# Graph layer kernel: tile 5 transposed by DMA, two adjacency chunks loaded as halves between transposes, h of tiles 6 and 7 a step earlier

## The reference, cut to what matters

```python
# x: 2048 x 512, adj: 2048 x 2048 (sparse, diagonal filled), weight: 512 x 512
h = maximum(layernorm(x), 0)
h_q = round(minimum(h / a, 1) * 15)                    # 4 bit activations
w_q = round(abs(clip(w_norm / wa, -1, 1)) * 7) * sign  # w_norm: weight, centred and scaled
support = relu(h_q @ w_q * scales)
s_q = round(minimum(support / a2, 1) * 15)
x = x + (adj @ s_q) * scales
h = maximum(layernorm(x), 0)
# attention over listed pairs, masked by an aggregator that is the identity
# for adj without ones: its softmax picks the row itself
x = x + h
```

## Time and profile before

| | |
|---|---|
| median of 3 runs | 151.84 us (151.78 to 152.19) |
| the profiled execution | 152.06 us, span 150.2 us |
| PE busy | 135.2 us, 90% of the span |
| DVE / ACT / POOL busy | 107.8 / 103.4 / 35.1 us |
| the chain that ended last | PE 74%, DVE 7%, issue 6%, DMA 2% |

### The profile page before, as it was taken

The page is one execution under the profiler, slowest core; times in us unless marked ns, Lnnn a source line. Parts: engine busy times, 40 slices in busy tenths (PEclk is TensorE's granted clock), DMA queues, the critical chain, the costliest instruction groups (busy, mean ns, idle before and its releaser), DMA issues.

```text
span 150.2 us, 2087 instructions
## 1 busy us (share of the span) xinstructions
PE 135.2 (90%) x672; PEld 85.5 (57%) x676; DVE 107.8 (72%) x223; ACT 103.4 (69%) x153; POOL 35.1 (23%) x72
## 2 busy tenths in 40 slices
PE   0397999799999999999999999999999999999920
PEld 0393545355555555757484757565666657579920
DVE  0889978699865569996863686686968797765450
ACT  3688785678686779506955999999999779411000
POOL 2565412243040000025100201101010652611010
PEclk9999999999999999999999999999999999999996
DMA  5999999531571780250189899999011021011102
GB/s 150 354 395 419 404 398 392 81 70 37 155 231 39 214 380 0 35 249 0 13 286 412 238 393 373 367 357 343 30 60 70 0 74 70 0 70 70 70 9 72
DMA packets 12925, 27.70 MB, mean 184 GB/s; under 512 B 6128, under 2 KB 6384, under 8 KB 10864
## 3 DMA queue, kind: packets, MB, share of 16 engines
q1 hardware_dynamic: 12624, 27.14, 51.7%
q10 hardware_dynamic: 288, 0.39, 0.8%
HBM read 22.03 MB, written 4.19 MB: 175 GB/s over the span
## 4 chain that ended last, share of the span: by engine, by line
PE 74%; DVE 7%; issue 6%; DMA 2%; ACT 1%; POOL 1%; POOLq 0%; DVEq 0%; ACTq 0%
PE acc L1078 27%; PE acc L1074 25%; PE acc L1040 8%; PE acc L1058 7%; PE acc L1053 6%; DVE st L787 2%; DMA h_iT<-h_i 2%; ACT z_sup L453 1%; DVE h_qT L827 1%; ACT h_i L445 1%; DVE ring L861 1%; POOL rs L582 1%; DVE x_sb L983 1%; DVE mv L792 0%; DVE sup L832 0%
## 5 line engine op out<-in xcount | busy, mean ns | idle before, releaser
L1078 PE MATMUL acc<-sup,lo 128*128 128x512 f32 (+1 forms) x208 | 48.3, 384 | 0.0
L1074 PE MATMUL acc<-sup_h,hi 128*128 128x512 f16 (+1 forms) x208 | 43.7, 363 | 0.0
L1078 PEld LDWEIGHTS acc<-sup,lo 128*128 128x128 f32 x208 | 37.0, 188 | 7.9
L567 POOL TENSOR_SCALAR nm<-mv 128x1 f32<-128x1 f32 (+2 forms) x19 | 13.2, 692 | 96.1 <-DVE ve L797 78.0
L426 ACT ACTIVATE junk<-raw,below 128x2048 uint8<-128x2048 f32 x16 | 31.8, 1988 | 0.0
L1074 PEld LDWEIGHTS acc<-sup_h,hi 128*128 128x128 f16 x208 | 19.4, 98 | 21.4 <-issue 2.9
L843 DVE TENSOR_TENSOR lo<-raw,hi 128x2048 fp32r<-128x2048 f32 x11 | 25.2, 2288 | 7.5 <-ACT hi L418 7.5
L460 ACT ACTIVATE ring<-x_sb,nm 128x512 f32<-128x512 f32 x15 | 10.4, 715 | 20.4 <-POOL nm L567 17.2
L1058 PE MATMUL acc<-sup,lo 128*128 128x512 f32 x64 | 21.7, 450 | 0.0
L418 ACT ACTIVATE hi<-raw 128x2048 f16<-128x2048 f32 x11 | 20.9, 1896 | 0.0
L787 DVE BATCH_NORM_STATS2 st<-x_sb 128x6 f32<-128x512 f32 x29 | 19.4, 688 | 0.4
(11 more groups left out here) (77 smaller groups left out, 82.3 us busy)
## 6 DMA issues: line engine op xcount, KB each, us to landing
raw<-adj_t SPq DMA_DIRECT2D x16, 1024.0 KB, 5.8
out<-ring SPq DMA_DIRECT2D x15, 256.0 KB, 4.7
x_sb<-x SPq DMA_DIRECT2D x3, 1024.0 KB, 13.9
w_sb<-weight SPq DMA_DIRECT2D x4, 258.0 KB, 4.0
x_sb<-x SPq DMA_DIRECT2D x1, 512.0 KB, 5.6
x_sb<-x ACTq DMA_DIRECT2D x1, 256.0 KB, 3.6
x_sb<-x SPq DMA_DIRECT2D x1, 256.0 KB, 4.7
h_iT<-h_i SPq DMA_TRANSPOSE x10, 2.5
```

What stands on the lines that cost most here:

```text
L567: nc.gpsimd.tensor_scalar(nm[:, a:a + m], mv[:, a:a + m, 0], -1.0, None, ALU.mult).then_inc(nm_ready, 1)
L1074: nc.tensor.matmul(bank[:, cols], part(hi, k % PARTS, j), sup_h[:, j, cols], start=(j == 0), stop=False)
L1078: ins = nc.tensor.matmul(bank[:, cols], part(lo, k % PARTS, j), sup[:, j, cols], start=False, stop=(j == T - 1))
```

## The change

It has four parts. (1) TURN = 5: tile 5 is transposed by DMA too, and the loop of transposes on SP starts at tile 5. (2) Chunk 2 of adj, x of tiles 12 to 15 and chunk 3 are no longer issued ahead of all transposes. Chunks 2 and 3 are loaded as halves of 512 KB, with a semaphore for the first half; they go behind the transposes of tiles 5, 6, 8 and 10, and the last quarter of x goes behind that of tile 7. (3) AHEAD = 6: h of tiles 6 and 7 is made one step earlier on ACT, and on DVE the statistics of tile 6 move ahead of quantise_sup(2), and `normalise(6)` ahead of lo_of_piece(4). (4) For the last tile EPS is added to the statistics of the first half, so that POOL takes the root straight from `mv` and the variance instruction goes; and the two final stores change engines: ACT stores the first half, SP the second.

```diff
@@ -48,12 +48,13 @@
     HEADS = 8
     DK = D // HEADS
     EARLY = 2
-    TURN = 6
-    AHEAD = 8
+    TURN = 5
+    AHEAD = 6
     SLOTS = 4
 
     WARM_SUMS, WARM_FIRST, WARM_T = 16, 4, (18, 0)
     RAW = 7
+    HALVED = (2, 3)
     PARTS = 3
     RING = 4
 
@@ -157,6 +158,7 @@
         x_in = [sem(f"x_in{n}") for n in range(len(x_loads))]
         w_in = [sem(f"w_in{k}") for k in range(KD)]
         adj_in = [sem(f"adj_in{b}") for b in range(RAW)]
+        adj_half = [sem(f"adj_half{b}") for b in range(RAW)]
         const_ready = sem("const_ready")
         half_ready = sem("half_ready")
         ident_zero = sem("ident_zero")
@@ -178,6 +180,7 @@
         x_var = sem("x_var")
         var_ready = sem("var_ready")
         nm_ready = sem("nm_ready")
+        last_var = sem("last_var")
         r_ready = sem("r_ready")
         relu_ready = sem("relu_ready")
         nb_ready = sem("nb_ready")
@@ -327,13 +330,19 @@
                     sp.wait_ge(screened, k - RAW + 1)
                 sp.dma_start(raw[:, k % RAW, :], adj_t[k]).then_inc(adj_in[k % RAW], 16)
 
+            def load_half(k, first):
+
+
+                cols = slice(0, CHUNK // 2) if first else slice(CHUNK // 2, CHUNK)
+                sp.dma_start(raw[:, k % RAW, cols], adj_t[k][:, cols]).then_inc(adj_half[k % RAW] if first else adj_in[k % RAW], 16)
+
             def store(t):
 
                 if t < T - 1:
                     sp.wait_ge(out_ready, t + 1)
                 else:
-                    sp.wait_ge(last_out_ready, 1)
-                cols = slice(0, D) if t < T - 1 else halves[0]
+                    sp.wait_ge(last_out_ready, 2)
+                cols = slice(0, D) if t < T - 1 else halves[1]
                 sp.dma_start(out[t * P:(t + 1) * P, cols], ring[:, t % RING, cols]).then_inc(out_stored[t % RING], 16)
 
             for k in range(KD):
@@ -344,15 +353,18 @@
             load_x(3)
             load_adj(1)
             load_x(4)
-            load_adj(2)
-            load_x(5)
-            load_adj(3)
             for j in range(TURN, T):
                 wait_h(sp, j)
                 if j >= TURN + 2:
 
                     wait_hT(sp, j - 2)
                 sp.dma_start_transpose(h_iT[:, j % 2, :, :], h_i[:, j % SLOTS, :]).then_inc(h_turned[j % 2], 16)
+                if j in (5, 6):
+                    load_half(2, j == 5)
+                if j == 7:
+                    load_x(5)
+                if j in (8, 10):
+                    load_half(3, j == 8)
                 if j == 11:
 
                     load_adj(GT)
@@ -405,8 +417,13 @@
             def split_piece(p):
                 k, q = p // 4, p % 4
                 if q == 0:
-                    act.wait_ge(adj_in[k % RAW], 16 * (k // RAW + 1))
+                    if k in HALVED:
+                        act.wait_ge(adj_half[k % RAW], 16)
+                    else:
+                        act.wait_ge(adj_in[k % RAW], 16 * (k // RAW + 1))
                     wait_part_free(act, k)
+                if q == 2 and k in HALVED:
+                    act.wait_ge(adj_in[k % RAW], 16)
                 cols = slice(q * PIECE, (q + 1) * PIECE)
                 nc.scalar.activation(hi[:, k % PARTS, cols], raw[:, k % RAW, cols], ACT.Copy,
                                      accum_out=low[:, p:p + 1]).then_inc(hi_piece, 1)
@@ -524,8 +541,8 @@
                     screen_ones(seen)
                     seen += 1
             assert seen == T
-            act.wait_ge(last_out_ready, 2)
-            act.dma_start(out[(T - 1) * P:, halves[1]], ring[:, (T - 1) % RING, halves[1]]).then_inc(out_stored[(T - 1) % RING], 16)
+            act.wait_ge(last_out_ready, 1)
+            act.dma_start(out[(T - 1) * P:, halves[0]], ring[:, (T - 1) % RING, halves[0]]).then_inc(out_stored[(T - 1) % RING], 16)
             with general(act):
                 one_ahead(act, (g_qk_ready, 1))
                 act.wait_ge(first_stored, 1)
@@ -630,8 +647,9 @@
                 n = FIRST + 1 + s - GT
                 centre(n, *second_ln[s - GT])
                 inverse_root(*second_ln[s - GT])
-            pool.wait_ge(var_ready, FIRST + len(second_ln) - EARLY)
-            inverse_root(T - 1, 1)
+
+            pool.wait_ge(last_var, 1)
+            nc.gpsimd.tensor_tensor(rs[:, T - 1:T], mv[:, T - 1, 1:2], minus_half[:, 0:1], ALU.pow).then_inc(r_ready, 1)
             with general(pool):
                 pool.wait_ge(first_stored, 1)
                 pool.wait_ge(g_var, 1)
@@ -922,20 +940,21 @@
             bound_hT(2)
             bound_hT(3)
             lo_of_piece(2)
+            stats(6)
             quantise_sup(2)
 
-            stats(6)
             normalise(5, stats(7))
             bound_hT(4)
             quantise_sup(3)
             lo_of_piece(3)
             wait_x(8)
             stats(8)
+            last = stats(9)
             bound_hT(5)
             quantise_sup(4)
+            normalise(6, last)
             lo_of_piece(4)
-            normalise(6, stats(9))
             bound_hT(6)
             quantise_sup(5)
             lo_of_piece(5)
@@ -985,15 +1004,20 @@
                     if s == T:
                         dve.wait_ge(x1_ready, a + n + 1)
                         ins = nc.vector.bn_stats(st[:, a + n, :], x_sb[:, t, cols])
+                        if n == 0:
+
+                            dve.wait_ge(dve_chain, step(ins))
+                            ins = nc.vector.tensor_scalar(st[:, a, 2:3], st[:, a, 2:3], float(D) * EPS, None, ALU.add)
+                            step(ins)
                 if s < T:
                     for t in range(a, a + m):
                         dve.wait_ge(x1_ready, t + 1)
                         ins = stats(t)
-                    after = mean_var(step(ins), a, m)
+                    variance(mean_var(step(ins), a, m), a, m)
                 else:
                     dve.wait_ge(dve_chain, step(ins))
-                    after = step(nc.vector.bn_aggr(mv[:, a, :], st[:, a:a + 2, :].rearrange("p h s -> p (h s)")))
-                variance(after, a, m)
+                    nc.vector.bn_aggr(mv[:, a, :], st[:, a:a + 2, :].rearrange("p h s -> p (h s)")).then_inc(last_var, 1)
+                    dve.wait_ge(last_var, 1)
                 if s == T:
                     last_result(a)
                     break
```

## The result

The kernel became slower: 154.31 us (153.86 to 155.17, 4 runs) against 152.01 us (151.78 to 152.33, 4 runs) for the kernel before, a ratio of 1.014 with a 95% interval of 1.011 to 1.017. Forecast were 150.7 us and a range of 149.9 to 152.0. The profiled execution took 154.66 us with a span of 152.9.

A forecast was written before the change was run, and what follows sets the result against it. PE's matmuls were taken to bound the kernel, with gains possible only before PE's steady pace and in the tail. First stage 0.76, root 0.18 and stores 0.2 sum to 1.14 us off 151.84: 150.7 us, range 149.9 to 152.0.

The forecast's parts named there:

- ACT's wait for nb: ACT ahead of h(6): a 1.3 us wait delays piece 4 and z_sup(4), hidden by 0.3 us before PE needs sup_h(4).
- PE's own path to support(6): First stage: PE is free at 28.08 after lo of tile 4 and starts support(6) at about 28.1, 1.1 us ahead.
- tile 5's transpose: First stage: by DMA it lands in 2.5 us, at 24.4, hidden with 0.3 us to spare; support(5) starts 0.56 us ahead.
- Support(4): First stage: with tile 6's statistics moved into DVE's idle time, support(4) starts at 22.35, not 22.89, 0.54 us won.
- Rival (c): Tile 5's DMA transpose takes 4.4 us, support(5) starts 1.1 us behind its old time, kernel 152.5 us; chance 0.04.
- the half load: First half of chunk 2, ahead of tile 6's transpose: lands 3.9 us after issue, at 27.05, the transpose at 27.6.
- the load of x and tile 8: x of tiles 12 to 15 ahead of tile 8's transpose: transpose lands at 33.35, leaving 0.76 us of first-stage gain.
- rival (b): Loads stream at lone pace, 3.6 us a megabyte; tile 8's transpose lands at 34.8, kernel 152.1 to 152.6 us; chance 0.08.
- (a): Rival: x's load takes up to 1 us longer, eating the first stage's gain; kernel 151.2 to 151.7 us; chance 0.22.
- tile 12: First stage after tile 8: only half loads between transposes; landings forecast for tiles 9 to 11, none for tile 12.
- the stores: Tail: exchanging the queues of the two final stores wins 0.2 us, bounds 0 and 0.5.
- the root: Tail: POOL's root, starting straight from the aggregation, begins at about 144.98, 0.18 us won.

## Why the prediction was wrong

**Right.** That the ends lie in the first stage's pace and the tail; that ACT's wait for nb would cost nothing (1.41 us, forecast 1.3, and free); PE's own path to support(6), which I had at 10.0 us behind support(2) and which took 10.02 with chunk 2 in front, where the transposes came in time; tile 5's transpose (2.9, 2.7 and 2.5 us forecast; support(5) won 0.36 us on its start, with 0.56 forecast). Support(4) won 0.31 us and not 0.54, measured from support(2). Rival (c) did not come in after, where no load is ahead of tile 5's transpose, and came to pass when the loads were put back in front: 5.3 us, PE waiting 2.5. The rule of the Trainium skill ("VectorE: DVE Perf Modes", "Rules for kernel authors"), TensorE where a PSUM destination will do, agrees with these runs. Tile 5's 2.9 us by DMA were hidden, but they bought nothing: support(6) came 10.02 us behind support(2) with tile 5 by DMA (chunk 2 in front), and 10.03 with it on PE (loads as in after, and the run with one load between transposes).

**Wrong, the half load.** I gave it 3.9 us. It took 4.5, so halving saved 0.8 us and not 1.3. Tile 6's transpose landed at 28.88, and with the start 0.52 later the forecast was 28.1. Of the 0.6 us that were then missing of the 1.1, PE's wait shows 0.43; the rest was missing at support(5) already.

**Wrong, the load of x and tile 8.** I took 33.35 for tile 8's landing. It was 35.27, so 1.4 us late against a start 0.52 later. The 33.35 took the pattern of the earlier trace rows, one load with one transpose behind it, with 0.4 us on top for a half load and a transpose in flight. No row stood under that 0.4, and it should have been 1.8: x took 7.0 us, 1.8 more than the lone load, with a half load and a transpose still slowly under way ahead of it. This is rival (b), just past its point of decision (34.6; with the start taken off, the landing is 34.75), and I had given it 0.08. It put the landing at 34.8, which with the later start is 35.3. That this fits so well is in part luck: the steps ahead of it were 0.5 to 1.0 us short (tile 7's transpose at about 30.8 by its prices, measured 31.79), and the 0.9 us that it took for a transpose's own streaming stands in no row; a lone transpose measured 0.66 us of the 16 engines' time (23.7% of 2.8 us, above). What I held against (a), that the queue isn't empty when x's load enters, went with a slower load and not a faster one. And x itself was late: I had it hold DVE at a place where DVE waits for tile 8's transpose anyway, and it held DVE longer than the transpose did, by 0.24 us.

**Wrong, no price at all, and the largest term: tile 12.** I stopped pricing at tile 11 and wrote that only half loads stand between transposes after tile 8. Chunk 4 was there before the change and no line of the diff moves it; with half of chunk 3 now issued 2.5 us ahead of it, it took 8.0 us instead of 5.2 and tile 12's transpose 7.1 instead of 4.4. PE, which before had its transpose at 44.1 for a support(12) at 45.25, waited 1.8 us. Taking chunk 4 away from there took the wait away. I had named "a wait at tile 9 or later" as what would prove me wrong, and given it no chance of its own.

**Wrong, the stores.** 0.2 us for an exchange that gives nothing; the root made up for it, 0.35 us where I had 0.18, since it also ran 0.55 us instead of 0.72. That the tail's total came near the forecast is luck.

The sum by these steps: the stage was to lose 0.76 us and gained 2.67, a miss of 3.4: 0.6 up to tile 6, 0.9 at tile 8, 1.9 at tile 12. The median rose by 2.3 us; 2.67 less the tail's 0.2 to 0.35 is about that.

**Open.** Why chunk 4 takes 7.6 to 8.0 us in after and with chunk 2 in front. The order half load, transpose, load, transpose is not enough: with tile 5 back on PE it is the same, and chunk 4 took 5.7. In the slow cases the load ahead, the second half of chunk 3, landed 1.8 to 2.5 us after chunk 4's issue, with tile 5 on PE 0.8 us after it, and with whole loads or chunk 4 later nothing of chunk 3 was in flight any more. That this overlap decides is my reading of six profiles; no run changed it alone. The windows show packets that stall in the middle; they don't show whether a transpose's small pieces hold up the load's or the other way round. A transpose with loads of other shapes beside it was not tried.
